# Cross-attention and soft-MoE kernel: the softmax reciprocals are spread over partitions by DMAs instead of by TensorE and ScalarE

## The reference, cut to what matters

```python
def xattn(x, context, Wq, Wk, Wv, Wo):          # B=8, N=56, M=1500, 16 heads of 64
    q, k, v = x @ Wq, context @ Wk, context @ Wv # split into heads
    sim = einsum('bihd,bjhd->bhij', q, k) * SCALE
    attn = softmax(sim, axis=-1)
    out = einsum('bhij,bjhd->bihd', attn, v)
    return out.reshape(B, N, INNER) @ Wo
x = x + xattn(layernorm(x), ctx_1024, ...)       # x is (8, 56, 128), ctx_1024 is (8, 1500, 128)
x = x + soft_moe(layernorm(x), phi_w, phi_b, expert_w, expert_b)
```

## Time and profile before

| | |
|---|---|
| runs, median (lowest to highest) | 487.86 us (487.70 to 487.96), n = 3 |
| span of the profiled execution | 483.5 us |
| median of the runs less this span | 4.36 us |
| mean granted TensorE clock | 0.979 of full speed |
| PE busy | 441.9 us (91%) |
| DVE busy | 359.2 us (74%) |
| ACT busy | 256.8 us (53%) |
| POOL busy | 120.6 us (25%) |
| `spread_rden` on PE (L603) | 56 instructions, 8.7 us busy |
| `copy_rbc` on ACT (L1034) | 16 instructions, 8.6 us busy |

### The profile page before, as it was taken

The page is one execution under the profiler, slowest core; times in us unless marked ns, Lnnn a source line. Parts: engine busy times, 40 slices in busy tenths (PEclk is TensorE's granted clock), DMA queues, the critical chain, the costliest instruction groups (busy, mean ns, idle before and its releaser), DMA issues.

```text
span 483.5 us, 7391 instructions
## 1 busy us (share of the span) xinstructions
PE 441.9 (91%) x2776; PEld 384.6 (80%) x2776; DVE 359.2 (74%) x600; ACT 256.8 (53%) x439; POOL 120.6 (25%) x55
## 2 busy tenths in 40 slices
PE   2899899999999999999999999999999995865767
PEld 2788788898899889988988897889878875565657
DVE  2467776777786777768666877675799999999780
ACT  1466566665564556656565565663666640325532
POOL 0507000503050022305000503050123428434250
PEclk9999999999999999999999999999999999778899
DMA  7110100010010001000100021000000009800000
GB/s 214 42 64 1 66 1 0 1 65 0 2 42 24 1 0 66 0 0 2 61 0 0 30 85 37 1 1 1 0 2 0 1 0 276 159 0 2 1 1 20
DMA packets 8496, 15.38 MB, mean 32 GB/s; under 512 B 291, under 2 KB 4275, under 8 KB 8469
## 3 DMA queue, kind: packets, MB, share of 16 engines
q1 hardware_dynamic: 6996, 12.91, 9.2%
q10 hardware_dynamic: 1472, 2.10, 1.5%
HBM read 14.78 MB, written 0.23 MB: 31 GB/s over the span
## 4 chain that ended last, share of the span: by engine, by line
PE 69%; DVE 22%; DMA 4%; ACT 3%; issue 1%; POOL 0%; SPq 0%; DVEq 0%
PE turned L575 14%; PE scores L563 7%; PE scores L565 7%; PE scores L564 7%; PE acc L593 7%; PE acc L595 7%; PE acc L594 7%; DVE csum L1359 3%; PE misc L507 3%; DMA ctx_raw<-in_ctx_dram 3%; DVE bankmax L1290 3%; DVE cmax L1342 2%; DVE pT_l L1299 2%; PE misc L609 2%; PE misc L501 2%; DVE disp L1377 2%
## 5 line engine op out<-in xcount | busy, mean ns | idle before, releaser
L1299 DVE TENSOR_TENSOR pT_l<-turned,pT_h 125x512 fp32r<-125x512 f32 x168 | 112.2, 688 | 65.8 <-ACT pT_h L1019 65.3
L1019 ACT CAST pT_h<-turned 125x512 fp32r<-125x512 f32 x168 | 95.3, 592 | 112.6 <-PE turned L575 112.4
L1290 DVE TENSOR_REDUCE bankmax<-scores 128x1 f32<-128x500 f32 x168 | 110.5, 675 | 20.6 <-PE scores L565 20.3
L575 PEld LDWEIGHTS turned<-ident,prob 128*125 128x125 f32 x672 | 88.3, 187 | 14.7 <-DVE pT_l L1299 8.5
L575 PE MATMUL turned<-ident,prob 128*125 128x128 f32 x672 | 94.4, 276 | 2.4 <-DVE pT_l L1299 2.2
L1026 ACT ACTIVATE prob<-scores,negmax 128x1500 f32<-128x1500 f32 x56 | 85.1, 1520 | 9.9 <-DVE negmax L1293 9.8
L593 PE MATMUL acc<-pT_h,ctx_nh 125*128 125x384 f32 (+1 forms) x192 | 78.2, 407 | 0.0
L595 PE MATMUL acc<-pT_h,ctx_nl 125*128 125x384 f32 (+1 forms) x192 | 70.1, 365 | 0.0
L594 PE MATMUL acc<-pT_l,ctx_nh 125*128 125x384 f32 (+1 forms) x192 | 69.9, 364 | 0.0
L563 PE MATMUL scores<-ctx_th,qk_h 128*128 128x500 f32 x168 | 69.2, 412 | 0.6 <-DVE qk_l L1283 0.3
L385 POOL TENSOR_TENSOR ctx_nh<-ctx_raw,zero 125x1536 fp32r<-125x1536 f32 x8 | 22.0, 2748 | 184.4 <-PE acc L595 169.3
(11 more groups left out here) (169 smaller groups left out, 581.1 us busy)
## 6 DMA issues: line engine op xcount, KB each, us to landing
ctx_raw<-in_ctx_dram SPq DMA_DIRECT2D x7, 750.0 KB
eb<-in_L_ffn_expert_b_dram SPq DMA_DIRECT2D x4, 256.0 KB, 8.0
ctx_raw<-in_ctx_dram SPq DMA_DIRECT2D x3, 250.0 KB
wq_sb<-in_L_xattn_Wq_dram ACTq DMA_DIRECT2D x1, 512.0 KB, 5.2
wk_sb<-in_L_xattn_Wk_dram ACTq DMA_DIRECT2D x1, 512.0 KB, 8.6
wv_sb<-in_L_xattn_Wv_dram ACTq DMA_DIRECT2D x1, 512.0 KB, 9.1
wo_sb<-in_L_xattn_Wo_dram ACTq DMA_DIRECT2D x1, 512.0 KB, 15.0
x_sb<-in_x_dram SPq DMA_DIRECT2D x1, 224.0 KB, 5.7
```

The source lines that it names most:

```text
L575: last = tr(turned[0:CK, m, 128 * c:128 * c + 128], prob[u][:, CK * j:CK * j + CK], ident[:, :])
L1019: nc.scalar.copy(pT_h[0:CK, t, CPB * k:CPB * k + CPB, :], turned[0:CK, (KB * u + k) % 2, :].rearrange("p (c r) -> p c r", c=CPB)).then_inc ...
L1290: m = v.tensor_reduce(bankmax[:, u, k:k + 1], scores[:, k, 0:KW], AX.X, ALU.max)
L1299: v.tensor_tensor(pT_l[0:CK, t, dst, :], turned[0:CK, (KB * u + k) % 2, :].rearrange("p (c r) -> p c r", c=CPB), pT_h[0:CK, t, dst, :].bit ...
```

## The change

SP now takes the reciprocals from `rden` to `rbc` through a DRAM tensor `rden_row`, with two DMAs for each of the 16 groups. The first writes `rden` (128 partitions x 3 or 4 values) transposed, each value of four bytes at its own place. SP waits for it to land, waits for `normalise` of the group before, and issues the second, which reads the row of 384 or 512 values to each of the 128 partitions. `normalise` waits for this load. `spread_rden` on PE and `copy_rbc` on ACT are gone, and the waits of PE that were tied to them are replaced by waits for what else used the same bank. SP's loop is written out, since the DMAs of the groups stand between the loads of the context; in it the `phi_w` load is issued before `spread_rden(12)`, and that before the `phi_b` loads. In the tail one wait of PE moves to just before `logits(2, 3)`.

```diff
+        rden_row = nc.dram_tensor("rden_row", [2, 128, 4], F32, kind="Internal").ap()
...
+            def spread_rden(n, a, grp):
+
+                t0, t1 = GROUPS[grp]
+                w = t1 - t0
+                row = rden_row[grp].rearrange("r t -> (r t)")[0:128 * w]
+                sp.wait_ge(rden_dve, n)
+                sp.dma_start(row.rearrange("(t r) -> r t", t=w), rden[:, a * NT + t0:a * NT + t1],
+                             allow_slow_non_contiguous=True).then_inc(rden_out, 16)
+                sp.wait_ge(rden_out, 16 * n)
+                wait(sp, oT_dve, n - 1)
+                sp.dma_start(rbc[:, 0:128 * w], row.partition_broadcast(128)).then_inc(rbc_in, 16)
+
+            def half(b, a, first=False):
+
+                if not first:
+                    spread_rden(2 * b, 1 - a, 1)
+                load_ctx(b + 2)
+                spread_rden(2 * b + 1, a, 0)
+
             load_ctx(1)
-            with sp.Fori(1, PAIRS) as i:
-                load_ctx(2 * i)
-                load_ctx(2 * i + 1)
...
+            half(0, 0, first=True)
+            half(1, 1)
+            for i in range(1, LAST):
+                half(2 * i, 0)
+                half(2 * i + 1, 1)
             sp.wait_ge(qk_pe, 4 * PAIRS)
             sp.dma_start(phi_sb[:, :, :], phi_w.rearrange("(k p) d -> p k d", p=128)).then_inc(phi_in, 16)
+            spread_rden(2 * (B - 2), 1, 1)
             sp.wait_ge(bias_zero, 1)
...
+            spread_rden(2 * (B - 2) + 1, 0, 0)
+            spread_rden(2 * (B - 1), 0, 1)
+            spread_rden(2 * B - 1, 1, 0)
+            spread_rden(2 * B, 1, 1)
             sp.wait_ge(pv_pe, 2 * B)
...
-            def spread_rden(a, grp, m):
-
-                t0, t1 = GROUPS[grp]
-                for t in range(t0, t1):
-                    last = tr(misc[:, m, 128 * (t - t0):128 * (t - t0) + 128],
-                              rden[:, a * NT + t:a * NT + t + 1].broadcast_to([128, 128]), ident[:, :])
-                last.then_inc(rbc_pe, 1)
...
-            pe.wait_ge(rden_dve, 2 * B)
-            spread_rden(1, 1, 1)
             turn_probs(G - 1, 1, 2)
...
+            pe.wait_ge(logit_act, 2 * LC + 3)
             logits(2, 3)
...
-            def copy_rbc(n, grp, m):
-                act.wait_ge(rbc_pe, n)
-                wait(act, oT_dve, n - 1)
-                w = 128 * (GROUPS[grp][1] - GROUPS[grp][0])
-                nc.scalar.copy(rbc[:, 0:w], misc[:, m, 0:w]).then_inc(rbc_act, 1)
...
             def normalise(n, a, grp):
 
-                dve.wait_ge(rbc_act, n)
+                dve.wait_ge(rbc_in, 16 * n)
                 dve.wait_ge(pv_pe, n)
```

More of the change, by code:

```diff
@@ L232, in xattn_softmoe_kernel @@
         rden_dve = sem("rden_dve")
-        rbc_pe = sem("rbc_pe")
-        rbc_act = sem("rbc_act")
+        rden_out = sem("rden_out")
+        rbc_in = sem("rbc_in")
         oT_dve = sem("oT_dve")
@@ L649, in early @@
                 if step == (0, 0, True):
-                    pe.wait_ge(rbc_act, 2 * b - 1)
+                    pe.wait_ge(qk_lo, 4 * PAIRS - 1)
                     pe.wait_ge(y_act, 2)
@@ L660, in early @@
                 if step == (0, 2, True):
-                    pe.wait_ge(rbc_act, 2 * b)
+                    pe.wait_ge(x1_dve, 1)
                     turn_phi(2, M0)
@@ L682, in early @@
                 if step == (1, 0, False):
-                    pe.wait_ge(rbc_act, 2 * b - 1)
+                    pe.wait_ge(logit_act, 2)
                     logits(0, 3)
@@ L688, in early @@
                 if step == (1, 2, True):
-                    pe.wait_ge(rbc_act, 2 * b)
+                    pe.wait_ge(logit_act, LC)
                     logits(1, 0)
@@ L791, in half @@
                         make_qk(i + 1, 0, 0)
[L792 to L797, removed]
                     if 2 <= t <= 4 and not last and not first:
@@ L802, in half @@
                         elif k == 1:
-                            wait(pe, rbc_act, b * 2)
+                            pe.wait_ge(ctxT_lo, KB * b + 3)
                         elif a == 0:
@@ L822, in half @@
                         project(0)
[L823 to L835, removed]
+                    if t == 6 and a == 0 and not first:
+                        project(1).then_inc(y_pe, 1)
                     if ending:
@@ L880, in _ @@
             turn_probs(G - 1, 1, 1)
-            pe.wait_ge(logit_act, 2 * LC + 3)
-            pe.wait_ge(rden_dve, 2 * B)
-            spread_rden(1, 1, 1)
             turn_probs(G - 1, 1, 2)
@@ L895, in _ @@
             slots_in(0, 1)
-            pe.wait_ge(rbc_act, 2 * B)
             slots_in(0, 2)
@@ L1148, in half @@
                         hi_qk(i + 1, 0, 0)
-                    if t == 1 and not first:
-                        copy_rbc(b * 2, 1, a)
                     if 2 <= t <= 4 and not last and not first:
@@ L1154, in half @@
                         hi_qk(i + 1, t - 3, (t - 3) % 2)
[L1155 to L1158, removed]
+                    if t == 6 and a == 0 and not first:
+                        copy_y(i - 1)
                     if ending:
@@ L1181, in _ @@
             hi_probs(G - 1, 1, NT - 1, 2)
-            copy_rbc(2 * B, 1, 1)
             dispatch_exp(1)
```

## The result

The changed kernel takes 502.12 us (median of four runs, 499.74 to 505.02), the kernel before 487.78 us (487.63 to 487.96) beside it: ratio 1.0315, 95% interval 1.0256 to 1.0374. It is slower by 14.3 us, where 5.0 us less were forecast, and it lies far outside the forecast range of 481.5 to 485.8 us. A second set of four runs on another chip gave 501.97 us against 488.09 us, 1.0296 (1.0262 to 1.0330).

What follows compares the result with a forecast made beforehand. PE was taken to bound the kernel until 368 us, then mostly DVE. Removing spreads gives 1.98 + 2.64 + 0.4 = 5.0 us with all round trips hidden: 487.86 - 5.0 = 482.9 us, range 481.5 to 485.8.

Steps and rivals of the forecast that it cites:

- the price W of the store: Landing time of the first DMA, rden to DRAM: 2.3 us for three tiles, 2.7 for four, upper bound 5.7.
- The second DMA: Broadcast load of the DRAM row into rbc: taken as 2.2 us, at most 5.7.
- the removal: Spread instructions taken off PE's path: 1.98 us odd groups, 2.64 even, 0.4 for n = 14, sum 5.0 us.
- 0.33 and 0.44 us per group: Path time on PE of one spread of three or four instructions, at 0.11 us per instruction.
- group 1: The spread of n = 1, three instructions in the PE stretch: counted as a gain of 0.33 us.
- n = 11: Spread at the end of half 5, before PE's wait for the phi load: its removal gives nothing.
- rival D: PE's freed time becomes waits for lo_probs or exp_tile: 485.9 us, or 487.9 if no group gains; chance 0.06.
- rival E: More gain than counted: n = 11, 15 and 16 count too, 6.1 us in all, 481.8 us; chance 0.08.
- three thresholds: Lateness costs time beyond 6.2 us round trip at normalise(15), 4.6 us store for phi, some 12 us in the steady state.
- Rival C: Slower: dearer store pieces delay normalise(15) and phi; at an 8 us store 7.7 us lost, 490.6 us; chance 0.08.
- R: Round trip of store, SP's 0.3 us and load: 4.8 us, 5.2 for four tiles, at most 11.7.
- SP is free for phi if ... W < 4.6 us: On SP, group 11's store precedes phi: no cost below 4.6 us, each further us costs PE one us.

Runs made afterwards that it cites:

- in rows: Changed kernel with all stores keeping rden's layout (each partition's 3 or 4 values side by side), normalise reading with a stride: 481.98 us against 487.38 before, ratio 0.9908.
- one tile side by side: Changed kernel storing only each group's first tile, 128 four-byte pieces within 512 bytes, loads reading Wq, output not the reference's: 489.13 us, one run.
- without any spread: Changed kernel without the 16 stores and 16 loads, rbc loaded once from Wq, output not the reference's: 482.31 us against 487.38 before, ratio 0.9896.
- the second execution: The changed kernel unaltered, run again on another chip as yardstick: 501.97 us against 488.09 us for the kernel before, ratio 1.0296.

## Why the prediction was wrong

**The step that failed** is the price W of the store: "I take 2.3 and 2.7: the warm stores are nearest in kind and direction". It measured 8.0 and 8.2 us, beyond the upper bound of 5.7 us too. Both bounds came from rows whose pieces are 512 bytes. The lower one scales with the count of pieces, and the count isn't what this store pays for: 1.7 and 1.8 us with as many pieces 64 bytes apart. The layout was in the diff, `"(t r) -> r t"` with r on the partitions, and was counted as many small pieces only, not as many writers of the same 64 bytes. The Trainium skill (DMA: Bandwidth & Descriptors, Rules for kernel authors) says of a strided last dimension that it costs one descriptor per element, and that one should rearrange. The advice was right here: in rows the store lands in 2.1 and 1.4 us. The count doesn't explain the 8 us: as many pieces of four bytes landed in 1.7 us.

**The second DMA**, taken as 2.2 us without a row of its kind, took 4.7 or 4.8: mis-sized also, within its bound of 5.7. It lands in 3.8 or 3.9 us after a store in rows. From Wq it lands in 2.9 to 3.1 us after a store with its pieces apart, but the 256 KB took 4.4 us after a store of one tile side by side. So the source alone doesn't explain it, and the cause is open.

**Right: the removal.** 5.0 us predicted; without any spread 5.1 us in the medians (2.1 to 8.0) and 4.46 us in the milestones. Of the terms, 0.33 and 0.44 us per group hold within 0.09 us; group 1 gave nothing; phi took back 0.39 us where only n = 11's 0.33 was put at nothing. But for this, no freed time became waits (rival D), and the tail neither gained nor lost (rival E).

**Right: the places and their rooms, wrong their sum.** The prediction gave three thresholds: round trip 6.2 us at `normalise(15)`, W of 4.6 us for phi, some 12 us in the steady part. All three were passed, and each place lost time. Rival C named these two losses at a chance of 0.08, and put them at 490.6 us for W = 8 us; its reason, a dearer piece, is not what the runs show. (The chances hold a slip: "the rest of C, 0.09" is more than the whole of C.) The kernel without spread and the changed one have the same start in their profiles, and their spans differ by 503.1 - 482.3 = 20.8 us. The staircase divides it, for this pair of executions:

| place | by rival C, W = 8 us | measured | what the rival's sum lacked |
|---|---|---|---|
| steady part | 0 | 1.8 us | round trips of 12.4 to 12.7 us against rooms of 12.1 and less (`normalise` of 1, 3 and 7) |
| phi, half 6 | 3.4 us | 10.5 us | this store took 9.6 us; the load lands 4.3 us later once issued; PE's clock |
| tail | 4.3 us | 8.5 us | the dearer load, R = 12.9 in place of 10.5; PE's clock |

Of phi's 10.5 us, 8.8 us are the longer wait (10.4 less 1.6 us) and 1.7 us the scores at half clock; of the tail's 8.5 us, 7.0 are the stall and 1.5 what follows at half clock. The extra at phi came back in the second execution (1.6 us). The tail's did not: there it lost 5.8 us, for a stall of 6.4. So a wait of PE in a stretch that it bounds is paid again in slower matmuls after it, and no step of the prediction had that; in the tail, which DVE bounds, no such price is shown.

Why the phi load lands later stays open. A broadcast load is ahead of it, 0.5 us old at its issue; with that load 3.4 us older (all in rows) phi landed in 6.5 us. But with one tile side by side that load was 0.5 us old too, and phi landed in 6.97 us. What is behind it is a rival: SP issues the slow store of group 12 at 295.49 us, 3.2 us after phi. The queues are then idle for the last 4 us before phi lands at 303.03 us:

```profile
299.00:303.00 4.00, 0.00 (x0) 0.00 (x0) 0.00 (x0) 0.00 (x0) 0.00 (x0) 0.50 0.00 0
```

The store itself has landed by 303.99 us. In the two other runs with a late phi (11.1 and 11.8 us) it is the same: idle queues, and phi 0.7 and 0.5 us ahead of the store. Where that store was issued only after phi had landed, phi took 6.5 or 6.6 us. No run moves this store alone, and the one-tile run, whose shorter store of group 12 took 5.8 us and did not delay phi, leaves room for another cause.

**Moved on SP.** "SP is free for phi if ... W < 4.6 us" was the right condition. Its cost came out larger than a us per us of W: of the 8.8 us by which PE's wait grew, some 4.5 are phi's later issue and 4.3 its later landing.

## What to carry to other kernels

Before pricing a small store, look at which bytes in DRAM its pieces share: here stores of four-byte pieces cost 6.3 us more with sixteen pieces to 64 bytes and 0.8 us more with four than with one. The same bytes kept in the source's layout landed in 1.4 to 2.1 us, and the reader's access pattern reordered them, at 862 ns in place of 610 for a `normalise`. A round trip through a queue that also carries a needed load is priced with all that stands behind its wait, and where PE bounds the kernel, a stall of it is priced with the slower matmuls after it (1.7 us at phi here). When a change frees time on the bound, as 5 us here, try its parts apart: all of the gain and a loss four times as large were in one kernel, and a line of layout told them apart.

## What the runs showed of the hardware that was not expected

- 128 to 512 four-byte pieces stored side by side land in 7.0 to 8.2 us, at 16 bytes' distance in 2.5 or 2.6, at 32 in 1.9 or 2.0, at 64 and 512 in 1.7 or 1.8 us; a store of 128 pieces of 12 bytes in 2.1, of 16 bytes in 1.4 us. In the 8 us of a slow store the queues are busy for about one, at a share of 0.20.
- A broadcast load of 192 or 256 KB from 1.5 or 2 KB of DRAM takes 2.9 to 3.1 us from an input, 4.4 us for 256 KB from the same input in the run with one tile side by side, 3.8 or 3.9 us from a row stored just before in rows and 4.7 or 4.8 us from one stored transposed.
- The first 27 us come in two kinds, some 3.2 us apart. Of the thirteen profiles six have their first `negmax` at 25.3 to 25.9 us, seven at 28.8 to 29.1, with and without the slow stores. In the slow kind the first score matmuls are spaced 0.41 us, as where the granted clock reads 0.54, though this stretch's reading is 1.00. What sets the kind is not known. Second and third score matmul and the window (columns as above) of the changed kernel, then the two matmuls of the kernel before:

```profile
25.93 0.62 PE L589 MATMUL scores<-ctx_tl,qk_h 128*128 128x500 f32 x1
26.34 0.62 PE L590 MATMUL scores<-ctx_th,qk_l 128*128 128x500 f32 x1
```

```profile
22.00:27.00 5.00, 5.00 (x21) 4.75 (x21) 0.78 (x2) 1.85 (x6) 1.17 (x1) 1.00 0.17 55
```

```profile
23.03 0.38 PE L564 MATMUL scores<-ctx_tl,qk_h 128*128 128x500 f32 x1
23.25 0.39 PE L565 MATMUL scores<-ctx_th,qk_l 128*128 128x500 f32 x1
```
